# Causal masking by GpSimd instead of TensorE, and a reordered DMA queue, in a transformer layer kernel on one core

## The chip, the cores and the metric

The kernel runs on one core of one Trainium2 chip. The metric is device time in microseconds of the whole program, the median of several runs. The engines of a core are TensorE (PE in the profile, with PEld for its weight loads), VectorE (DVE), ScalarE (ACT), GpSimd (POOL) and SyncE (SP), which here only issues DMAs.

## The reference

One layer with modulated norms: attention with 16 heads of 32 over 4 batches of 1024 tokens and 512 features, then a gated feed-forward block of 2048 hidden features, all in float32. What matters here is the attention:

```python
scores = einsum('bhqd,bhkd->bhqk', qn, kn) / sqrt(hd)      # qn, kn: rotated, normalised heads
scores = where(causal, scores, finfo.min)
w = softmax(scores, axis=-1)
a = einsum('bhqk,bhkd->bhqd', w, v)
```

## The kernel before

The program is four stages one after the other: `qkv_stage`, `attention_stage`, `project_stage`, `ffn_stage`. Only `attention_stage` is touched.

It works on 16 groups (`NG`), each one batch and four heads. For a group, q and k are transposed on TensorE (`prepare`), widened by ScalarE (`widen`, into `whole`), split in a high and a low float32r part by GpSimd (`high`) and VectorE (`low`), and copied by 12 DMAs of 256 KB (`lay_stacks`, L705) into a stack whose rows let one matmul multiply both parts. A first pass of matmuls (`score`, L803) gives scores of which VectorE takes the maximum of each query (`peak`, L888 and L891); the maxima are transposed and laid as two more rows of the stack (`lay_peaks`). A second pass (`shift`, L821) gives scores less their maximum, keys on partitions and queries along the free axis, in PSUM tile `psB` with two buffers; ScalarE takes the exponential into `probT` (`exponent`, L961, three buffers of four heads); and TensorE multiplies it by v and by ones (`weigh`, L839), into `psO` and `psL`. Keys come in 8 blocks of 128 and queries in 2 halves of 512: 12 pairs (`BLOCKS`), of which 8 contain the diagonal. On those, `shift` adds a matmul of the mask with the identity (L824) to the 128 columns on the diagonal, in the same PSUM tile.

All engines walk the same list of steps k. `unit(k)` gives the round n and the step w from 0 to 11 in it. In round n, step w, the scores of group n are taken, two items a step. The shifts run 14 steps (`SHIFT_LAG`) behind, so block 0 of a group is shifted in step 2 of the round after; steps 2 to 5 and 10, 11, 0, 1 shift blocks on the diagonal, steps 6 to 9 blocks without it. A step on TensorE is: two shifts, four score matmuls, two shifts, then `prepare` (steps 1 and 3, for the group after), the transposition of maxima (step 0), then `weigh` of the block that was shifted one step earlier. The third shift waits for the first exponential of its step, the fourth for the second, since `psB` has two buffers. Score tiles and `prepare` share two slots of `psA`; a slot is free when VectorE (or ScalarE) has read what was in it.

SyncE's order in a round: `lay_peaks` in step 0, in step 4 `load` (q and k of the group two further) and all 12 transfers of `lay_stacks`, in step 5 `load_v`, in step 10 `store`. SyncE isn't held to the steps; only its waits hold it. On GpSimd `normalise` does, for each group but the last, in step 3 of the round two after the group's scores: one DMA of the four rows of sums to DRAM (L759), one back as a 128x32 tile (L761), a wait for VectorE's reciprocal (L937, step 8), one DMA of the inverses to DRAM (L763), four that broadcast them to 128 partitions (L766), and the product with the attention output (L769). GpSimd stands in `normalise` until all is done.

Of the kernel before, what the change touches and what calls it, by code (L numbers as in the profile page):

```python
# [20 lines left out]
F32 = mybir.dt.float32  # L21
# [556 lines left out]
def attention_stage(nc, args, scratch):  # L578
# [12 lines left out]
    BUFS = 3  # L591

# [19 lines left out]
    def weigh_at(k):  # L612
        return shift_at(k - 1)

# [16 lines left out]
    with ExitStack() as ctx:  # L631
# [3 lines left out]
        def sem(name):  # L635
# [20 lines left out]
        probT = sb("b_probT", [P, 3, 4, W])  # L656
# [9 lines left out]
                 "peaks_turned peaks_copied peaks_in shifted expd weighed summed taken_o taken_l sums_out few_in inverted few_out "  # L666
# [17 lines left out]
        def _(sp):  # L684
# [15 lines left out]
            def lay_stacks(n):  # L700
                at_least(sp, s["shifted"], 4 * NW * (n - BUFS + 1))
                sp.wait_ge(s["lo_done"], 2 * n + 2)
                for j in range(4):
                    for r, pair in enumerate((slice(0, 4, 3), slice(2, 4), slice(0, 2))):
                        sp.dma_start(stack[r * HD:(r + 1) * HD, n % BUFS, :, j].bitcast(F32),  # L705
                                     halves[j * HD:(j + 1) * HD, pair].bitcast(F32)).then_inc(stack_in[j], 16)
# [14 lines left out]

            load(0)
# [4 lines left out]
            for k in STEPS:  # L727
                n, w = unit(k)
                if peaks_at(k) is not None:
                    lay_peaks(peaks_at(k))  # L730
                if w == 4 and n + 2 < NG:
                    load(n + 2)
                if w == 4 and n + 1 < NG:
                    lay_stacks(n + 1)
                if w == 5 and 0 <= n < NG:
                    load_v(n)
                if w == 10 and 0 <= n - 2 < NG:
                    store(n - 2)
            sp.wait_ge(stored, 16 * NG)

        @block.gpsimd
        def _(pool):
            make_identity(nc, pool, ident, s["ident_ready"])
            pool.memset(ones[:], 1.0).then_inc(s["k_ones"], 1)
            for n in range(BUFS):
                pool.wait_ge(s["k_ones"], 1 + n)
                pool.memset(stack[ROWS:NR, n, 0].bitcast(F32), 1.0).then_inc(s["k_ones"], 1)
            pool.wait_ge(s["k_ones"], 1 + BUFS)

            def high(n, m):  # L750
                pool.wait_ge(s["whole"], 2 * n + m + 1)
                if m == 0:
                    for j in range(4):
                        at_least(pool, stack_in[j], 48 * n)
                pool.tensor_scalar(halves[:, 3 if m else 0], whole[:], 1.0, 1.0, ALU.mult, ALU.mult).then_inc(s["hi_done"], 1)

            def normalise(n):
                pool.wait_ge(s["taken_l"], 2 * n + 2)
                pool.dma_start(scratch["sums"][0], sums[0:P:HD, n % 2]).then_inc(s["sums_out"], 16)  # L759
                pool.wait_ge(s["sums_out"], 16 * n + 16)  # L760
                pool.dma_start(few[:, 0], scratch["sums"][0].rearrange("j (a c) -> (j a) c", c=C // HD)).then_inc(s["few_in"], 16)  # L761
                pool.wait_ge(s["inverted"], n + 1)
                pool.dma_start(scratch["sums"][1].rearrange("j (a c) -> (j a) c", c=C // HD), few[:, 1]).then_inc(s["few_out"], 16)  # L763
                pool.wait_ge(s["few_out"], 16 * n + 16)
                for j in range(4):
                    pool.dma_start(sums[j * HD:(j + 1) * HD, n % 2], scratch["sums"][1, j:j + 1].broadcast_to([HD, C])).then_inc(s["wide_in"], 16)  # L766
# [12 lines left out]
        def _(pe):  # L779
# [32 lines left out]
            def shift(n, w, j):  # L812
# [10 lines left out]
                if first == kb:  # L823
                    mm = pe.matmul(psB[:, i % 2, 0:P], mask_r[:], ident_r[:], start=False, stop=True, skip_group_check=True)  # L824
                mm.then_inc(s["shifted"], 1)

            def weigh(n, w, summing):
                half, kb = BLOCKS[w]
                if not summing:
                    pe.wait_ge(s["expd"], 4 * (NW * n + w) + 4)  # L830
                    if w == 0:
                        pe.wait_ge(s["v_in"], 16 * n + 16)
# [4 lines left out]
                for j in range(4):  # L837
                    rows = slice(j * HD, (j + 1) * HD)
                    mm = pe.matmul(out[rows, (first - half * HALF) * P:W], ones[:] if summing else v[:, n % 2, kb, rows],  # L839
                                   probT[:, (NW * n + w) % 3, j, 0:(half + 1) * W - first * P],  # L840
# [21 lines left out]
        def _(dve):  # L862
# [60 lines left out]
            for k in STEPS:  # L923
# [19 lines left out]
        def _(act):  # L943
# [9 lines left out]
            def exponent(n, w, j):  # L953
# [7 lines left out]
                act.activation(probT[:, (NW * n + w) % 3, j, 0:width], psB[:, i % 2, 0:width], ACT.Exp).then_inc(s["expd"], 1)  # L961
# [498 lines left out]
```

## Time and profile before

| | us |
|---|---|
| median of 3 runs | 2434.78 (2433.34 to 2436.04) |
| the profiled execution | 2436.47 |
| its span | 2434.3 |
| attention stage, within the span | about 400 to 1208 |
| TensorE busy | 2242.7 (92%) |
| VectorE, ScalarE, GpSimd busy | 1200.8, 792.2, 728.7 |

The span is from the first to the last instruction. Busy times of TensorE count a matmul from issue to the modelled end of its pipeline, so that neighbours overlap.

### The profile page before, as it was taken

Reading aid. Unit: us, or ns where it says so; the run is one execution under the profiler, and the core shown is the slowest. Engines: PE = TensorE matmul, PEld = TensorE weight load, DVE = VectorE, ACT = ScalarE, POOL = GpSimd, SP = SyncE. Lnnn points to the kernel's source line nnn. Section 1 sums busy time; section 2 is a strip of 40 time slices with the busy share of each in tenths; the row PEclk is TensorE's granted clock in tenths of the full one; section 3 lists DMA queues with packets and bytes.
Section 4 is the critical chain, followed back from the end, with each engine's and each line's share of the span. In section 5 each row is a group of like instructions: output and inputs, shape, how many; then the busy total and the mean of one; then the engine's idle time right before and its main releaser. Section 6 shows DMA issues by size and latency. Waiting matters only on the chain. (4 is left out here: it accounts for less than half of the span.)

```text
span 2434.3 us, 32672 instructions
## 1 busy us (share of the span) xinstructions
PE 2242.7 (92%) x12008; PEld 1649.6 (68%) x12008; DVE 1200.8 (49%) x2775; ACT 792.2 (33%) x1671; POOL 728.7 (30%) x694
## 2 busy tenths in 40 slices
PE   6999993799999999999678799999999999999998
PEld 3777771455555555555356588888888888888887
DVE  5999995566665665665279512222222222221212
ACT  3333331155555555555445411111111111111111
POOL 2677775002112112111277122222222222222221
PEclk8999996599999999999899899999999999999999
DMA  6222223555465465452288411212121211111111
GB/s 225 70 96 94 103 87 120 118 134 132 102 152 126 107 151 130 107 128 76 68 256 303 161 52 52 70 48 69 52 69 49 66 56 65 52 64 37 52 53 52
DMA packets 161834, 243.71 MB, mean 100 GB/s; under 512 B 17124, under 2 KB 84292, under 8 KB 161184
## 3 DMA queue, kind: packets, MB, share of 16 engines
q1 hardware_dynamic: 153184, 220.66, 31.0%
q0 software_dynamic: 7456, 18.07, 2.6%
q10 hardware_dynamic: 1056, 3.15, 0.3%
q8 instruction: 87, 1.43, 0.2%
q14 instruction: 51, 0.42, 0.1%
HBM read 131.69 MB, written 59.26 MB: 78 GB/s over the span
## 5 line engine op out<-in xcount | busy, mean ns | idle before, releaser
L1324 DVE TENSOR_TENSOR f_gu<-f_psU,f_silu 128x512 f32<-128x512 f32 x128 | 88.6, 692 | 712.3 <-PE f_psU L1391 712.3
L961 ACT ACTIVATE b_probT<-b_psB 128x512 f32<-128x512 f32 (+3 forms) x768 | 339.4, 490 | 300.0 <-PE b_psB L824 220.9
L891 DVE TENSOR_REDUCE b_top<-b_psA 128x2 f32<-128x1024 f32 (+2 forms) x320 | 288.6, 902 | 134.0 <-PE b_psA L803 133.8
L1280 POOL TENSOR_SCALAR f_wd_hi<-f_wd 128x512 fp32r<-128x512 f32 x128 | 83.4, 652 | 819.7 <-PE f_psD L1376 775.9
L821 PE MATMUL b_psB<-b_stack 98*128 98x512 f32 (+3 forms) x768 | 273.6, 401 | 5.1 <-ACT b_probT L961 4.6
L821 PEld LDWEIGHTS b_psB<-b_stack 98*128 98x128 f32 x768 | 141.4, 189 | 156.0 <-issue 103.2
L1300 ACT ACTIVATE f_silu<-f_psG 128x512 f32<-128x512 f32 x128 | 76.5, 598 | 504.2 <-PE f_psG L1391 504.2
L803 PE MATMUL b_psA<-b_stack 96*128 96x512 f32 (+3 forms) x768 | 193.5, 373 | 35.8 <-DMA b_stack<-b_halves 20.1
L1389 PE MATMUL f_psG<-f_hT_hi,w_hi 128*128 128x512 f32 x512 | 200.4, 391 | 11.0 <-DVE f_hT_lo L1318 11.0
L1391 PE MATMUL f_psG<-f_hT_lo,w_hi 128*128 128x512 f32 x512 | 199.9, 390 | 0.0
L1390 PE MATMUL f_psG<-f_hT_hi,w_lo 128*128 128x512 f32 x512 | 199.9, 390 | 0.0
L1295 ACT ACTIVATE f_gu_hi<-f_gu 128x512 fp32r<-128x512 f32 x128 | 80.9, 632 | 364.5 <-DVE f_gu L1324 364.5
L1390 PE MATMUL f_psU<-f_hT_hi,w_lo 128*128 128x512 f32 x512 | 199.2, 389 | 0.0
L1391 PE MATMUL f_psU<-f_hT_lo,w_hi 128*128 128x512 f32 x512 | 199.2, 389 | 0.0
L1389 PE MATMUL f_psU<-f_hT_hi,w_hi 128*128 128x512 f32 x512 | 199.2, 389 | 0.0
L1374 PE MATMUL f_psD<-f_wd_hi,f_gu_hi 128*128 128x512 f32 x512 | 199.2, 389 | 0.0
L1375 PE MATMUL f_psD<-f_wd_lo,f_gu_hi 128*128 128x512 f32 x512 | 199.2, 389 | 0.0
L1376 PE MATMUL f_psD<-f_wd_hi,f_gu_lo 128*128 128x512 f32 x512 | 199.2, 389 | 0.0
L803 PEld LDWEIGHTS b_psA<-b_stack 96*128 96x128 f32 x768 | 136.2, 200 | 65.9 <-issue 22.6
L1282 POOL TENSOR_TENSOR f_wd_lo<-f_wd,f_wd_hi 128x512 fp32r<-128x512 f32 x128 | 168.8, 1319 | 10.7
L839 PE MATMUL b_psO<-b_probT,b_v 128*32 128x512 f32 (+3 forms) x1536 | 165.4, 503 | 0.0
L839 PE MATMUL b_psL<-b_probT,b_ones 128*32 128x512 f32 (+3 forms) x1536 | 159.0, 486 | 0.0
(178 smaller groups left out, 4084.4 us busy)
## 6 DMA issues: line engine op xcount, KB each, us to landing
b_stack<-b_halves SPq DMA_DIRECT2D x192, 256.0 KB, 5.1
f_wd<-in_wd_t SPq DMA_DIRECT2D x128, 256.0 KB, 2.6
qkv_d<-a_t SPq DMA_DIRECT2D x32, 512.0 KB, 2.7
b_land<-qkv_d SPq DMA_DIRECT2D x32, 512.0 KB, 4.7
a_x<-in_x SPq DMA_DIRECT2D x32, 256.0 KB, 3.3
qkv_d<-a_v SPq DMA_DIRECT2D x32, 256.0 KB, 3.1
b_v<-qkv_d SPq DMA_DIRECT2D x16, 512.0 KB, 5.8
att_d<-b_att SPq DMA_DIRECT2D x16, 512.0 KB, 3.2
```

The costliest lines, as they stand in the source:

```text
L803: mm = pe.matmul(out[:, h, 0:hi - lo], stack[0:ROWS, n % BUFS, 1, j, t * P:(t + 1) * P], stack[0:ROWS, n % BUFS, 0, j, lo:hi], start=True, ...
L821: mm = pe.matmul(psB[:, i % 2, cols], stack[0:NR, n % BUFS, 0, j, kb * P:(kb + 1) * P], stack[0:NR, n % BUFS, 1, j, first * P:(half + 1) * ...
L839: mm = pe.matmul(out[rows, (first - half * HALF) * P:W], ones[:] if summing else v[:, n % 2, kb, rows], probT[:, (NW * n + w) % 3, j, 0:(h ...
L891: last = dve.tensor_reduce(into, tile[:, :, 0:width], AX.X, ALU.max, negate=True)
L961: act.activation(probT[:, (NW * n + w) % 3, j, 0:width], psB[:, i % 2, 0:width], ACT.Exp).then_inc(s["expd"], 1)
L1282: pool.tensor_tensor(wd_lo[:, u % 2], wd[:, u % 2], wd_hi[:, u % 2].bitcast(F32), ALU.subtract).then_inc(s["wd_lo"], 1)
L1374: pe.matmul(out_t, gu_hi[:, u % 2, cols], wd_hi[:, u % 2], start=first, stop=False)
L1375: pe.matmul(out_t, gu_hi[:, u % 2, cols], wd_lo[:, u % 2], start=False, stop=False)
L1376: mm = pe.matmul(out_t, gu_lo[:, u % 2, cols], wd_hi[:, u % 2], start=False, stop=end)
L1389: pe.matmul(out_c, w_hi[:, m, k, cols], hi, start=(k == 0), stop=False)
L1390: pe.matmul(out_c, w_lo[:, m, k, cols], hi, start=False, stop=False)
L1391: mm = pe.matmul(out_c, w_hi[:, m, k, cols], lo, start=False, stop=(k == KC - 1))
```

## The change

In the diagonal blocks the mask matmul is gone. ScalarE takes the exponential of the unmasked values, and GpSimd clears those above the diagonal in `probT` with one `affine_select` over the four heads' 128x128 squares (`cut`); `weigh` waits for the cut in diagonal blocks, and for the exponential in the others. The DMAs of `normalise` move from GpSimd's queue to SyncE's, with their waits; what is left on GpSimd is the wait for the broadcast and the product, now in two halves, in step 10. VectorE's reciprocal moves from step 8 to 7. `lay_stacks` is called once a head from steps 4 to 7, `load_v` goes from step 5 to 7, `store` from step 10 to step 1 of the round after. `PROBS = 3` names the number of `probT` buffers, which stays.

```diff
+    DIAGONAL = [w for w, (half, kb) in enumerate(BLOCKS) if kb >= half * HALF]
+    def cut_at(k):
+        at = shift_at(k)
+        return at if at and at[1] in DIAGONAL else None
...
-            def lay_stacks(n):
-                at_least(sp, s["shifted"], 4 * NW * (n - BUFS + 1))
-                sp.wait_ge(s["lo_done"], 2 * n + 2)
-                for j in range(4):
-                    for r, pair in enumerate((slice(0, 4, 3), slice(2, 4), slice(0, 2))):
-                        sp.dma_start(stack[r * HD:(r + 1) * HD, n % BUFS, :, j].bitcast(F32),
-                                     halves[j * HD:(j + 1) * HD, pair].bitcast(F32)).then_inc(stack_in[j], 16)
+            def lay_stacks(n, j):
+                if j == 0:
+                    at_least(sp, s["shifted"], 4 * NW * (n - BUFS + 1))
+                    sp.wait_ge(s["lo_done"], 2 * n + 2)
+                for r, pair in enumerate((slice(0, 4, 3), slice(2, 4), slice(0, 2))):
+                    sp.dma_start(stack[r * HD:(r + 1) * HD, n % BUFS, :, j].bitcast(F32),
+                                 halves[j * HD:(j + 1) * HD, pair].bitcast(F32)).then_inc(stack_in[j], 16)
...
+            def sums_out(n):
+                sp.wait_ge(s["taken_l"], 2 * n + 2)
+                sp.dma_start(scratch["sums"][0], sums[0:P:HD, n % 2]).then_inc(s["sums_out"], 16)
+            def few_in(n):
+                sp.wait_ge(s["sums_out"], 16 * n + 16)
+                sp.dma_start(few[:, 0], scratch["sums"][0].rearrange("j (a c) -> (j a) c", c=C // HD)).then_inc(s["few_in"], 16)
+            def few_out(n):
+                sp.wait_ge(s["inverted"], n + 1)
+                sp.dma_start(scratch["sums"][1].rearrange("j (a c) -> (j a) c", c=C // HD), few[:, 1]).then_inc(s["few_out"], 16)
+            def wide_in(n):
+                sp.wait_ge(s["few_out"], 16 * n + 16)
+                for j in range(4):
+                    sp.dma_start(sums[j * HD:(j + 1) * HD, n % 2], scratch["sums"][1, j:j + 1].broadcast_to([HD, C])).then_inc(s["wide_in"], 16)
...
-                if w == 4 and n + 1 < NG:
-                    lay_stacks(n + 1)
-                if w == 5 and 0 <= n < NG:
+                if 0 <= n - 2 < NG - 1 and w in (4, 5, 8, 9):
+                    {4: sums_out, 5: few_in, 8: few_out, 9: wide_in}[w](n - 2)
+                if 4 <= w < 8 and n + 1 < NG:
+                    lay_stacks(n + 1, w - 4)
+                if w == 7 and 0 <= n < NG:
                     load_v(n)
-                if w == 10 and 0 <= n - 2 < NG:
-                    store(n - 2)
+                if w == 1 and 0 <= n - 3 < NG:
+                    store(n - 3)
...
+            def cut(n, w):
+                pool.wait_ge(s["expd"], 4 * (NW * n + w) + 4)
+                square = probT[:, (NW * n + w) % PROBS, :, 0:P]
+                pool.affine_select(out=square, in_=square, compare_op=ALU.is_ge, fill=0.0, base=0,
+                                   pattern=[[0, 4], [1, P]], channel_multiplier=-1).then_inc(s["cut"], 1)
             def normalise(n):
-                (the seven DMAs with their waits)
                 pool.wait_ge(s["wide_in"], 64 * n + 64)
                 pool.wait_ge(s["taken_o"], 2 * n + 2)
-                pool.tensor_tensor(att[:, n % 2], att[:, n % 2], sums[:, n % 2], ALU.mult).then_inc(s["scaled"], 1)
+                for half in range(2):
+                    cols = slice(half * W, (half + 1) * W)
+                    mul = pool.tensor_tensor(att[:, n % 2, cols], att[:, n % 2, cols], sums[:, n % 2, cols], ALU.mult)
+                mul.then_inc(s["scaled"], 1)
             for k in STEPS:
+                if cut_at(k):
+                    cut(*cut_at(k))
                 if prep_at(k):
                     high(*prep_at(k))
-                at = take_at(k)
-                if at and at[1] == 1 and at[0] < NG - 1:
-                    normalise(at[0])
+                n, w = unit(k)
+                if w == 10 and 0 <= n - 2 < NG - 1:
+                    normalise(n - 2)
...
-                if first == kb:
-                    mm = pe.matmul(psB[:, i % 2, 0:P], mask_r[:], ident_r[:], start=False, stop=True, skip_group_check=True)
...
-                    pe.wait_ge(s["expd"], 4 * (NW * n + w) + 4)
+                    if w in DIAGONAL:
+                        pe.wait_ge(s["cut"], len(DIAGONAL) * n + DIAGONAL.index(w) + 1)
+                    else:
+                        pe.wait_ge(s["expd"], 4 * (NW * n + w) + 4)
...
-                at = take_at(k - 5)
-                if at and at[1] == 1 and at[0] < NG - 1:
-                    dve.wait_ge(s["few_in"], 16 * at[0] + 16)
+                n, w = unit(k)
+                if w == 7 and 0 <= n - 2 < NG - 1:
+                    dve.wait_ge(s["few_in"], 16 * (n - 2) + 16)
                     dve.reciprocal(few[:, 1], few[:, 0]).then_inc(s["inverted"], 1)
```

## Rows read from the trace of the kernel before

**Rows 1.** Window of 50 us; busy PE, PEld, DVE, ACT, POOL, PEclk, DMA share, GB/s.

```profile
630.00:680.00 50.00, 48.57 (x369) 29.11 (x367) 31.83 (x109) 28.32 (x61) 8.12 (x10) 1.00 0.57 136
```

**Rows 2.** Timeline of SyncE's DMA issues: loads, stacks and v, and the next loads.

```profile
621.48 1.00 SPq L693 DMA_DIRECT2D b_land<-qkv_d  x2
625.22 13.72 SPq L705 DMA_DIRECT2D b_stack<-b_halves  x12
638.99 1.23 SPq L698 DMA_DIRECT2D b_v<-qkv_d  x1
...
667.20 1.00 SPq L693 DMA_DIRECT2D b_land<-qkv_d  x2
```

**Rows 3.** Timeline of TensorE: start us, us, instruction, [idle before <- releaser]; transposes.

```profile
612.26 1.06 PE L788 MATMUL b_psA<-b_ident,b_land 128*128 128x128 f32 x8 [0.44 <-DVE b_top L891]
...
620.36 1.09 PE L788 MATMUL b_psA<-b_ident,b_land 128*128 128x128 f32 x8 [0.66 <-DVE b_top L891]
```

**Rows 4.** Timeline of TensorE: starts of steps 1, 9, 10, 11, and weighings.

```profile
609.90 0.33 PE L821 MATMUL b_psB<-b_stack 98*128 98x128 f32 x1
...
610.40 1.02 PE L803 MATMUL b_psA<-b_stack 96*128 96x384 f32 x4
...
640.12 0.73 PE L821 MATMUL b_psB<-b_stack 98*128 98x512 f32 x2
640.70 0.87 PE L803 MATMUL b_psA<-b_stack 96*128 96x512 f32 x4
...
642.23 1.07 PE L839 MATMUL b_psO<-b_probT,b_v 128*32 128x512 f32 x8
...
644.08 0.50 PE L821 MATMUL b_psB<-b_stack 98*128 98x512 f32 x1
644.42 0.23 PE L824 MATMUL b_psB<-b_ident_r,b_mask_r 128*128 128x128 f32 x1
644.48 0.45 PE L821 MATMUL b_psB<-b_stack 98*128 98x512 f32 x1
...
644.83 1.03 PE L803 MATMUL b_psA<-b_stack 96*128 96x512 f32 x4
...
646.43 1.06 PE L839 MATMUL b_psO<-b_probT,b_v 128*32 128x512 f32 x8
...
648.28 0.44 PE L821 MATMUL b_psB<-b_stack 98*128 98x384 f32 x1
...
650.51 1.06 PE L839 MATMUL b_psO<-b_probT,b_v 128*32 128x512 f32 x8
...
654.19 0.85 PE L839 MATMUL b_psO<-b_probT,b_v 128*32 128x384 f32 x8
```

**Rows 5.** Timelines of VectorE and TensorE around the scores of step 5.

```profile
626.61 0.69 DVE L891 TENSOR_REDUCE b_top<-b_psA 128x2 f32<-128x512 f32 x1
...
627.07 1.14 PE L803 MATMUL b_psA<-b_stack 96*128 96x512 f32 x4
```

**Rows 6.** Timeline of the weight loads: the fourth shift of step 9.

```profile
641.79 0.19 PEld L821 LDWEIGHTS b_psB<-b_stack 98*128 98x128 f32 x1 [0.30 <-ACT b_probT L961]
```

**Rows 7.** Groups of GpSimd: busy us, mean ns | idle before: the select of 128x128.

```profile
L108 POOL TENSOR_SCALAR_AFFINE_SELECT b_ident<-b_ident 128x128 f32<-128x128 f32 x1 | 0.3, 294 | 0.1
```

**Rows 8.** Timeline of ScalarE: the last two exponentials of step 10.

```profile
646.19 1.09 ACT L961 ACTIVATE b_probT<-b_psB 128x512 f32<-128x512 f32 x2 [0.43 <-PE b_psB L824]
```

**Rows 9.** Window of 2 us, columns as in rows 1, while the stacks are transferred.

```profile
630.00:632.00 2.00, 2.00 (x23) 1.29 (x22) 1.58 (x10) 1.83 (x4) 0.00 (x0) 1.00 0.99 211
```

**Rows 10.** The instructions of L705, the stack transfers: from issue to landing.

```profile
DMA to landing us min/median/max: 3.2/5.1/7.1
```

**Rows 11.** Timeline of GpSimd: inverses out, broadcast in, product.

```profile
639.60 0.55 POOL L763 DMA_DIRECT2D sums_d<-b_few  x1 [11.85 <-DVE b_few L937]
643.12 1.98 POOL L766 DMA_DIRECT2D b_sums<-sums_d  x4 [2.97 <-DMA sums_d<-b_few]
647.62 2.38 POOL L769 TENSOR_TENSOR b_att<-b_att,b_sums 128x1024 f32<-128x1024 f32 x1 [2.53 <-DMA b_sums<-sums_d]
```

More of the change, by code:

```diff
@@ L591, in attention_stage @@
     BUFS = 3
+    PROBS = 3
     def unit(k):
@@ L655, in attention_stage @@
         peak_rows = sb("b_peak_rows", [8 * TB, P])
-        probT = sb("b_probT", [P, 3, 4, W])
+        probT = sb("b_probT", [P, PROBS, 4, W])
         sums = sb("b_sums", [P, 2, C])
@@ L665, in attention_stage @@
         names = ("mask_in ln_ready whole ident_ready consts k_ones qk_in v_in turned hi_done lo_done scored maxed peaks_ready "
-                 "peaks_turned peaks_copied peaks_in shifted expd weighed summed taken_o taken_l sums_out few_in inverted few_out "
+                 "peaks_turned peaks_copied peaks_in shifted expd cut weighed summed taken_o taken_l sums_out few_in inverted few_out "
                  "wide_in scaled end_inverted end_scaled").split()
@@ L755, in high @@
                 pool.tensor_scalar(halves[:, 3 if m else 0], whole[:], 1.0, 1.0, ALU.mult, ALU.mult).then_inc(s["hi_done"], 1)
-            def normalise(n):
[L758 to L766, printed above, removed]
+            def cut(n, w):
[3 more added lines that the diff above has]
+                                   pattern=[[0, 4], [1, P]], channel_multiplier=-1).then_inc(s["cut"], 1)
+            def normalise(n):
                 pool.wait_ge(s["wide_in"], 64 * n + 64)
                 pool.wait_ge(s["taken_o"], 2 * n + 2)
-                pool.tensor_tensor(att[:, n % 2], att[:, n % 2], sums[:, n % 2], ALU.mult).then_inc(s["scaled"], 1)
+                for half in range(2):
+                    cols = slice(half * W, (half + 1) * W)
+                    mul = pool.tensor_tensor(att[:, n % 2, cols], att[:, n % 2, cols], sums[:, n % 2, cols], ALU.mult)
+                mul.then_inc(s["scaled"], 1)
             for k in STEPS:
+                if cut_at(k):
+                    cut(*cut_at(k))
                 if prep_at(k):
                     high(*prep_at(k))
-                at = take_at(k)
-                if at and at[1] == 1 and at[0] < NG - 1:
-                    normalise(at[0])
+                n, w = unit(k)
+                if w == 10 and 0 <= n - 2 < NG - 1:
+                    normalise(n - 2)
         @block.tensor
@@ L839, in weigh @@
                     mm = pe.matmul(out[rows, (first - half * HALF) * P:W], ones[:] if summing else v[:, n % 2, kb, rows],
-                                   probT[:, (NW * n + w) % 3, j, 0:(half + 1) * W - first * P],
+                                   probT[:, (NW * n + w) % PROBS, j, 0:(half + 1) * W - first * P],
                                    start=(kb == 0), stop=(kb == (half + 1) * HALF - 1), skip_group_check=True)
@@ L960, in exponent @@
                 width = (half + 1) * W - max(kb, half * HALF) * P
-                act.activation(probT[:, (NW * n + w) % 3, j, 0:width], psB[:, i % 2, 0:width], ACT.Exp).then_inc(s["expd"], 1)
+                act.activation(probT[:, (NW * n + w) % PROBS, j, 0:width], psB[:, i % 2, 0:width], ACT.Exp).then_inc(s["expd"], 1)
             def copy_peaks(n):
```

## The prediction, made before the changed kernel ran

> **What bounds the kernel now.** I read the windows of the attention stage first, since every edit lies there (400 to 1205 us of the span). TensorE is busy 97% of a 50 us window, VectorE, ScalarE and GpSimd 64, 57 and 16%, at a granted clock of 1.00, the 2.4 GHz level [rows 1]. So TensorE's order of work sets the pace, but a busy TensorE row includes pipelining; what counts is where it waits, which the timeline tells. One round of twelve steps takes 45.7 us: SyncE's loads of step 4 are issued at 621.48 and at 667.20 [rows 2]. All times below are of the round from 609.90 to 655.6. TensorE waits for VectorE in it, 0.44 us before the transposes of step 1 and 0.66 us before those of step 3 [rows 3]. These two transpose blocks are 8.10 us apart (612.26 to 620.36), and between them lies a chain with no mask matmul in it: transposes, ScalarE widen, GpSimd high, VectorE low, VectorE maxima.
>
> **Mask matmuls removed.** 8 of 12 blocks are diagonal, 4 heads each, 16 groups: 512 matmuls with their weight loads. Price of one: in step 10 the two first shifts take 644.08 to 644.83, 0.75 us with two masks; the same pair without, in step 9, 640.12 to 640.70, 0.58 us [rows 4]. The stream itself is 0.06 us (644.42 to 644.48), the rest is its weight load. That is 0.09 us; narrower blocks, where the load weighs more, I put at 0.09 to 0.115 (the pair of 128 columns in step 1 takes 0.50 us, 609.90 to 610.40, and I put it at 0.27 without). Were TensorE alone the bound: 512 x 0.095 = 48.6 us. That is the upper end. The Trainium skill (TensorE: Matmul & The Clock Gate, Back-to-back issue gap) gives some 81 ns as the sustained spacing of a 128-column load-and-matmul pair, so 41.5 us by the page; the trace's 0.09 is near it; neither says how much is kept.
>
> How much is kept, step by step. Steps 2 and 3 and the second pair of step 1 (10 masks): nothing, they lie inside waits or inside the 8.10 us chain that VectorE ends. Step 1, first pair: 0.50 becomes 0.27, the scores, the maxima and the transposes move up by 0.23. Step 4: 0.38. Step 5: its first pair gains 0.19 more, but its second score, at 627.50 before (0.43 into the scores of 627.07), would be issued 0.61 earlier, and its PSUM slot is free only when the VectorE reduce of 626.61 ends (0.69 us, 627.30) [rows 5]. That chain starts at the transposes of step 3, so 0.14 is left at that point and the second pair adds 0.20: steps 4 and 5 keep 0.34. Steps 6 to 9 have no mask. Step 10: without masks the fourth shift waits for ScalarE as in step 9 (the weight load idles 0.30 us) [rows 6], and weighing starts 2.11 us after the step in place of 2.35: 0.24. Step 11: 384 columns, exponentials shorter, so ScalarE holds nothing; weighing 2.23 us after 648.28; I keep 0.36. Step 0: 0.30 of 0.38, the rest to the exponentials. Sum 0.34 + 0.24 + 0.36 + 0.30 + 0.23 = 1.47 us a round, 15 rounds: **22 us gained**. Beyond the last scores ScalarE sets the pace; I take 0 there.
>
> **GpSimd cuts added.** 128 of them, 4x128 elements a partition. A select of 128x128 took 0.294 us [rows 7]. Lower bound that row itself, upper four times it, 1.18; the element work grows by four and only the start is paid once, so I take 0.9, nearer to the upper end. TensorE now waits for the cut where it waited for the fourth exponential. What is queued behind that wait is all of TensorE's stream, and ScalarE and VectorE wait for that. But the weighing of a block comes a whole step later: the exponentials of step 10 end at 647.28 (646.19 + 1.09) and its weighing is at 650.51 [rows 4, 8], 3.2 us later, 2.6 without the masks between; step 0's end about as long before the weighing in step 1. So a cut of 0.9, even of 1.2, is hidden, if GpSimd is free. The cut goes ahead of `high`, but `high` waits for ScalarE's widen, 1.2 us long and behind the same exponentials: hidden too. The last block has no step behind it: 0.9 us once, I put the tail at +1.
>
> **Transfers moved to SyncE.** The DMA engines are full from 624 to 642 us (0.99 of their time and 211 GB/s at 630 to 632) [rows 9]. SyncE issues 2 loads at 621.48, 12 stack transfers at 625.22 taking 13.72 us together, v at 638.99 for 1.23 [rows 2]. SyncE is not paced by steps, only by its waits, so "four steps" is only an order: new is loads, `sums_out` (behind the loads), three stacks, `few_in` (wait passed), nine stacks, v, `few_out`, wait, four `wide_in`. `few_in` is issued near 627.6 and lands some 5.1 us later, the stacks' median [rows 10], near 633; the reciprocal, now in step 7, is reached near 635 (the inverses of step 8 left at 639.60, a step is 3.96): no wait. `few_out` in the kernel before was issued at 639.60 from GpSimd's own queue, as soon as VectorE's reciprocal was there, and the four `wide_in` followed at 643.12 [rows 11]. Now it waits for SyncE: 625.22 + 13.72 + 0.6 (`few_in`) + 1.23 = 640.8. It stands behind v in the same queue; the stack transfers there take 3.2 / 5.1 / 7.1 us from issue to landing, so 644.0 to 647.9, I take 645.9. From the first `wide_in` to the product it was 4.5 us (643.12 to 647.62), so the product starts near 650.4 in place of 647.62. It lasts 2.4 us (in two halves). **The new wait:** on GpSimd the product of step 10 stands ahead of the cut of step 11, and it waits for `wide_in`. So that cut runs 652.8 to 653.7. TensorE wants it in step 0: 654.19 before, less 0.34 + 0.24 + 0.36 + 0.30 = 652.95. It waits about 0.7 us a round, in the 13 rounds that have both a product and stack transfers: **9 us given back**. The other queue effects are covered: the stacks are needed a half round later, `lay_peaks` at 654.62 stands behind `wide_in` issued by 648, v is needed a round on, the store moved to step 1 has until step 7.
>
> The Trainium skill (DMA: Bandwidth & Descriptors, Queues, rings and completion order) says that an engine consumes one ring in order and takes turns between rings. By that rule small transfers behind megabytes on SyncE's queue wait for them, and on GpSimd's own queue they did not: 3.5 us for `few_out` (639.60 to 643.12) against 5.1 for a stack on the full queue agrees. It speaks against this part of the change.
>
> **Sum.** 2436.47 (profiled execution: span 2434.3 and 2.2 around it) - 22 + 9 + 1 = 2424.5. The median shown is 1.7 lower, so 2422.8; I say 2423.
>
> **Rivals.** (a) The landing is earlier, or the cut shorter by 0.3, and the wait at step 0 vanishes: 0.7 us is little against DMA spreads of 4 us. Then 2434.8 - 21 = 2414, and if step 5 and ScalarE hold back less than I say, 2404. For it: SyncE's four issues may be quicker than GpSimd's. Against: full DMA engines. (b) GpSimd, stuck at the product, becomes the bound. One wait, `wide_in` at step 10 ahead of the next cut: it decides from a product start of 651.2, where the stall eats the 1.47. If `few_out` takes the 7.1 us of the longest stack transfer, the product starts at 652.4: 2.7 us of wait a round, 13 x 2.7 = 35 against 21, 2449 us; with 6.2 us, 2438. For it: the ring order above. Against: the queue drains behind v. (c) The masks were wholly covered (VectorE and ScalarE chains already set each step) and the wait as well: 2433 to 2436, no change. Against: steps 4, 11 and 0 have no idle entry before their shifts or scores.
>
> **How the numbers follow.** A median of this kernel can be told apart from no change at about 0.2%, 5 us: faster is below 2429.9. Forecast (2416 to 2430, a wait of 0.2 to 1.3 us): 0.48. (a) 0.22. (c) 0.12. (b) 0.18. Range 2404 to 2442 takes in (a) whole and (b) up to a landing of 6.6 us, leaving out about 2 in 10. Faster 0.47 + 0.22 = 0.69, same 0.14, slower 0.17.
>
> **What would show it.** No row of a mask matmul; a pair of 512-column shifts at 0.56 to 0.60 us in step 10. The two transpose blocks of a round still 8.1 us apart. Cuts at 0.5 to 1.2 us. `few_out` issued after v, 15 to 16 us after the first stack, the product 25 us after the first stack. A wait of TensorE for the GpSimd cut once a round, at the weighing of step 0, near 0.7 us; if it is 0, (a), if above 1.5, (b). A round of 45.7 - 1.47 + 0.7 = 44.9 us. Wrong altogether: cuts over 2 us, a VectorE wait for `few_in`, or a TensorE wait at another cut.

## The result, and the profile after

The changed kernel took 2422.94 us (median of 6 runs, 2422.32 to 2426.79) against 2434.94 (6 runs, 2433.34 to 2436.04): a ratio of 0.9953, interval 0.9942 to 0.9964. The forecast was 2423. The size is right, and so is the 22 us gained; the reason given for the 9 us given back is not.

The profiled span is 2423.7 us. The first view is the page's table of busy times: TensorE is down from 2242.7 us (512 instructions fewer). GpSimd is up by 27: 81.1 us of cuts came, and 55.7 us of issuing the DMAs of `normalise` went. The second is the grouped view of two GpSimd lines, the cut and the product: how many, ns of one as least/median/most, and the first and last start.

```profile
PE 2211.0 (91%) x11496; PEld 1588.9 (66%) x11496; DVE 1207.5 (50%) x2775; ACT 790.4 (33%) x1671; POOL 755.8 (31%) x732
```

```profile
L786 POOL TENSOR_SCALAR_AFFINE_SELECT b_probT<-b_probT x128: 625/634/642, 479.6 to 1189.1; 128x512 f32<-128x512 f32 x128
...
L794 POOL TENSOR_TENSOR b_att<-b_att,b_sums x30: 1268/1280/1294, 558.7 to 1181.8; 128x512 f32<-128x512 f32 x30
```

TensorE's timeline after, answering to [rows 3, 4]: the two transposition blocks, and the two first shifts of step 10.

```profile
611.56 1.06 PE L816 MATMUL b_psA<-b_ident,b_land 128*128 128x128 f32 x8 [0.66 <-DVE b_top L920]
...
619.65 1.09 PE L816 MATMUL b_psA<-b_ident,b_land 128*128 128x128 f32 x8 [0.83 <-DVE b_top L920]
...
643.05 0.73 PE L849 MATMUL b_psB<-b_stack 98*128 98x512 f32 x2
643.62 0.98 PE L831 MATMUL b_psA<-b_stack 96*128 96x512 f32 x4
```

The blocks are still 8.09 us apart, with longer waits before them (0.66 and 0.83 for 0.44 and 0.66): what the masks of steps 1 to 3 cost inside that chain became waiting. The pair of step 10 takes 0.57 us, not 0.75.

SyncE's timeline after, answering to [rows 2, 11].

```profile
624.51 2.35 SPq L712 DMA_DIRECT2D b_stack<-b_halves  x3
626.91 1.17 SPq L735 DMA_DIRECT2D b_few<-sums_d  x1
628.13 10.04 SPq L712 DMA_DIRECT2D b_stack<-b_halves  x9
638.22 1.24 SPq L705 DMA_DIRECT2D b_v<-qkv_d  x1
639.50 1.47 SPq L739 DMA_DIRECT2D sums_d<-b_few  x1
644.88 1.72 SPq L744 DMA_DIRECT2D b_sums<-sums_d  x4
```

`few_out` went 15.0 us after the first stack transfer and the broadcast 5.4 us after it. Now the three engines at that place: GpSimd, then VectorE's gathering of the maxima (L926 to L933), then TensorE.

```profile
646.02 0.63 POOL L786 TENSOR_SCALAR_AFFINE_SELECT b_probT<-b_probT 128x512 f32<-128x512 f32 x1 [17.41 <-ACT b_probT L990]
649.14 2.52 POOL L794 TENSOR_TENSOR b_att<-b_att,b_sums 128x512 f32<-128x512 f32 x2 [2.48 <-DMA b_sums<-sums_d]
651.61 0.64 POOL L786 TENSOR_SCALAR_AFFINE_SELECT b_probT<-b_probT 128x512 f32<-128x512 f32 x1
```

```profile
649.69 0.96 DVE L920 TENSOR_REDUCE b_top<-b_psA 128x2 f32<-128x768 f32 x1
650.68 1.02 DVE L926 TENSOR_TENSOR b_least<-b_top 128x32 f32<-128x32 f32 x1
651.74 0.55 DVE L928 SCALAR_TENSOR_TENSOR b_least<-b_corner,b_least 128x32 f32<-128x32 f32 x1
652.32 0.18 DVE L931 CAST b_peaks<-b_least 128x32 fp32r<-128x32 f32 x1
652.54 0.19 DVE L933 TENSOR_TENSOR b_peaks<-b_least,b_peaks 128x32 fp32r<-128x32 f32 x1
652.66 0.29 DVE L917 CUSTOM_DVE_ANT_0 b_masked<-b_psA,b_mask 128x128 f32<-128x128 f32 x1
```

```profile
651.56 0.66 PE L849 MATMUL b_psB<-b_stack 98*128 98x256 f32 x2
653.32 0.30 PE L838 MATMUL b_psA<-b_ident,b_peaks 128*128 128x128 f32 x1 [1.10 <-DVE b_corner L917]
653.55 0.85 PE L868 MATMUL b_psO<-b_probT,b_v 128*32 128x384 f32 x8
```

The product starts 24.6 us after the first stack transfer, as forecast (25.2), and the cut behind it ends at 652.25. But TensorE stands somewhere else, one instruction earlier: at the transposition of the maxima (L838), for 1.10 us. Its weights are what L933 writes, and its PSUM slot comes free by maxima that VectorE takes behind L933. The four small operations of the gathering are late, and two of them are long: L926 took 1.02 us, and it ended when the second half of the product ended (651.7); L928 took 0.55 and ended with the cut. The grouped view of the same two lines shows what they took before (they are L897 and L899 there) and after, ns as least/median/most:

```profile
L897 DVE TENSOR_TENSOR b_least<-b_top x16: 191/191/216, 467.2 to 1154.4; 128x32 f32<-128x32 f32 x16
...
L899 DVE SCALAR_TENSOR_TENSOR b_least<-b_corner,b_least x16: 191/191/193, 467.5 to 1154.6; 128x32 f32<-128x32 f32 x16
```

```profile
L926 DVE TENSOR_TENSOR b_least<-b_top x16: 191/399/1024, 468.0 to 1144.6; 128x32 f32<-128x32 f32 x16
...
L928 DVE SCALAR_TENSOR_TENSOR b_least<-b_corner,b_least x16: 191/370/1205, 468.2 to 1144.8; 128x32 f32<-128x32 f32 x16
```

In the view of waits of the kernel after (total us, times, longest), this wait and the one that I had forecast:

```profile
PE b_psA L838 <- DVE b_corner L917: 7.7, 12, 1.8
...
PEld b_psO L868 <- POOL b_probT L786: 0.6, 1, 0.6
```

One of the twelve (0.6 us, in the first round) is there before too, so 7.1 us in 11 rounds are new; the wait for the cut came once. There is a second loss, seen in windows of 4 us (columns as in [rows 1]): in some rounds TensorE's granted clock falls.

```profile
528.00:532.00 4.00, 3.17 (x17) 1.96 (x20) 1.59 (x6) 1.84 (x3) 0.64 (x1) 0.61 0.02 7
532.00:536.00 4.00, 4.00 (x36) 1.81 (x28) 2.68 (x5) 1.48 (x5) 1.45 (x2) 0.96 0.92 270
```

The same engine, with the same work, stands near its lower level of 1.2 GHz (a granted clock of 0.5) for most of a window, after the waits around the transposition block of step 3. It isn't the new wait that comes before this fall: the transposition of the maxima at 517.00 waited for nothing. Such a round is 1.1 us longer here: 45.83 us from 517.00 to 562.83 with a wait of 0.27, against 44.93 from there to 607.76 with one of 0.47. The kernel before had two such falls (at 756 and 940 us, about 1.6 us each), this one has four (528, 664, 888, 980). All six come about 12 us behind the transposition of the maxima. Falls behind the last scores, where these kernels have one or none, are left out of all counts here.

### The profile page after: what moved, and what is told of

Read it like the earlier page. It is cut to its first block and busy times, and to the rows that moved or that the text cites. A ratio compares the mean times of both kernels' runs of the same rounds, so it can differ in the third digit from the quotient of the medians.

```text
span 2423.7 us, 31792 instructions
## 1 busy us (share of the span) xinstructions
PE 2211.0 (91%) x11496; PEld 1588.9 (66%) x11496; DVE 1207.5 (50%) x2775; ACT 790.4 (33%) x1671; POOL 755.8 (31%) x732
## 5 line engine op out<-in xcount | busy, mean ns | idle before, releaser
L849 PE MATMUL b_psB<-b_stack 98*128 98x512 f32 (+3 forms) x768 | 253.8, 397 | 6.8 <-ACT b_probT L990 6.8
L849 PEld LDWEIGHTS b_psB<-b_stack 98*128 98x128 f32 x768 | 131.1, 189 | 171.1 <-issue 106.5
L786 POOL TENSOR_SCALAR_AFFINE_SELECT b_probT<-b_probT 128x512 f32<-128x512 f32 x128 | 81.1, 634 | 486.6 <-ACT b_probT L990 486.6
```

The lines of the kernel that those rows point to most:

```text
L849: mm = pe.matmul(psB[:, i % 2, cols], stack[0:NR, n % BUFS, 0, j, kb * P:(kb + 1) * P], stack[0:NR, n % BUFS, 1, j, first * P:(half + 1) * ...
```

## The experiments

The ratios below are against the kernel before, run on the same chip. Theory P is that VectorE's gathering is held by GpSimd's instructions; Q is the prediction's own, queueing on GpSimd or a full DMA ring.

**Masks left out, nothing cleared.** The kernel before without its mask matmuls, to see what their removal alone is worth.

```diff
-                if first == kb:
-                    mm = pe.matmul(psB[:, i % 2, 0:P], mask_r[:], ident_r[:], start=False, stop=True, skip_group_check=True)
```

> The kernel before with the 512 mask matmuls left out and nothing in their place (values above the diagonal are not cleared); transfers and product stay where they were. It prices the mask matmuls alone. Prediction on record: 1.47 us kept in each of 15 rounds, 22 us, so 2413. Reading of the changed kernel's trace: 37.6 us from the transposes of step 3 to those of the next step 1 became 36.4 where nothing waited, 1.25 us a round, 19 us, so 2416; the 8.10 us from the transposes of step 1 to those of step 3 stay. If VectorE and ScalarE covered the masks wholly: 2433 to 2436. If TensorE alone set the pace: 2386.

2410.7 us (2409.63 to 2415.68), ratio 0.9907 (0.9891 to 0.9922). It is 24.3 us under before. A round takes 44.35 us in place of 45.70: 1.35 kept, where I summed 1.47. Over the 13 full rounds that is 17.6; the last, from the 15th transposition of maxima to the 16th, which has no chain with transposes, gives 2.4 (41.81 to 39.37), the first 1.8 (48.15 to 46.33; a part of this may be the clock, which comes back to its upper level in this round, at 483.5 us and not at 484.6), and the two falls of the clock are gone, 3.2. That is 25.0 of the 25.7 us between the two spans. The median lies under both forecasts above (2413 and 2416), since neither had the falls. So the changed kernel gives back 12 us of what removing masks is worth.

**Transfers alone.** The change, with the masks back and the cuts gone.

```diff
+                if first == kb:
+                    mm = pe.matmul(psB[:, i % 2, 0:P], mask_r[:], ident_r[:], start=False, stop=True, skip_group_check=True)
...
-                if cut_at(k):
-                    cut(*cut_at(k))
...
-                    if w in DIAGONAL:
-                        pe.wait_ge(s["cut"], len(DIAGONAL) * n + DIAGONAL.index(w) + 1)
-                    else:
-                        pe.wait_ge(s["expd"], 4 * (NW * n + w) + 4)
+                    pe.wait_ge(s["expd"], 4 * (NW * n + w) + 4)
```

> The changed kernel with the mask matmuls back and no cuts: only the transfers on SyncE, the reciprocal in step 7, the halved product in step 10 and the later store. Theory Q (what I forecast: the product, waiting for the broadcast, holds the next cut and TensorE waits for that cut): without cuts nothing waits, no change against before, within 2 us. Theory P (VectorE's two-input operations of the gather in step 0 are held while a GpSimd operation on SBUF runs): the product ends 27 us after the first stack transfer, the gather of a round with masks comes at about the same time (652.2 against 651.6 in the round I use), so a few rounds are hit by a part of an operation: 0 to 3 us slower. Q and P hardly differ here; the run tells whether the transfers cost anything without the cuts.

2434.54 us (2432.51 to 2436.65), ratio 0.9997 (0.9988 to 1.0006): the reordered queue alone neither gives nor takes. The product starts where it does in the change (649.53 us in this round, for 2.52), but with rounds of 45.7 us the gathering comes only at 652.25, 0.2 us behind its end; in 13 of 16 rounds its first operation takes 0.19 us. In two rounds TensorE waits for it, 0.18 and 0.11 us. So the late product does harm that counts only together with the shorter round.

**The product in step 2.** All of the change, but the product goes a third of a round later, to step 2, behind that step's cut, and the store with it to step 3. From the second round on, the last cut before the gathering then ends 0.3 us before it (in one round 602.86 and 603.18).

```diff
-                if w == 10 and 0 <= n - 2 < NG - 1:
-                    normalise(n - 2)
+                if w == 2 and 0 <= n - 3 < NG - 1:
+                    normalise(n - 3)
...
-                if w == 1 and 0 <= n - 3 < NG:
+                if w == 3 and 0 <= n - 3 < NG:
                     store(n - 3)
```

> The changed kernel, with the product of a group in step 2 of the round after, behind that step's cut, and its store in step 3. No cut stands behind a wait for the broadcast, and the product runs 34 us away from the gather. Theory Q: the wait of TensorE at the weighing of step 0 goes; as its trace shows only 0.6 us of that wait in all, 0 to 1 us faster than the changed kernel, 2422. Theory P: gather operations back at 0.19 us each, the waits of TensorE before the transposition of the maxima (7.1 us in all) go, 6 to 8 us faster than the changed kernel: 2415 to 2417. Against both: if the product delays the cut of step 3, a wait appears there.

2411.95 us (2410.63 to 2413.36), ratio 0.9905 (0.9889 to 0.992): 11 us under the changed kernel, more than P asked for. In the grouped view the gathering is back at 191 ns in all 16 rounds, and in the view of waits only the first round's entry is left:

```profile
L926 DVE TENSOR_TENSOR b_least<-b_top x16: 191/192/193, 466.2 to 1130.5; 128x32 f32<-128x32 f32 x16
...
L928 DVE SCALAR_TENSOR_TENSOR b_least<-b_corner,b_least x16: 191/191/193, 466.4 to 1130.7; 128x32 f32<-128x32 f32 x16
```

```profile
PE b_psA L838 <- DVE b_corner L917: 0.6, 1, 0.6
```

Rounds take 44.35 us again. It is within 1.3 us of the kernel that clears nothing, so the 128 cuts (81 us of GpSimd) cost nearly nothing by themselves (the profiled spans are 3.0 us apart, with one fall of the clock here in the full rounds and none there). Of the 12.1 us between this span (2411.6) and the changed kernel's, 7.1 are the waits, 1.2 some 0.11 us more in each of those 11 rounds, and 3.3 three falls of the clock more at 1.1 (this kernel has one).

**The cut first.** The product moved from step 10 to step 11, behind that step's cut. By the prediction's mechanism this is the cure: the cut waits for no transfer any more. By P it is the worst place, with both halves right beside the gathering.

```diff
-                if w == 10 and 0 <= n - 2 < NG - 1:
+                if w == 11 and 0 <= n - 2 < NG - 1:
                     normalise(n - 2)
```

> The changed kernel, with the product in step 11, behind the cut of that step in place of ahead of it. The one wait that theory Q is about is taken away: by Q 2422 or faster, down to 2414 if the forecast 0.7 us a round had been right. By theory P the product now begins after that cut, just when VectorE gathers the maxima, in every round: the gather's first operation is held 0.9 to 1.2 us and the second 1.0 to 1.3 us, TensorE waits 1.5 to 2.2 us a round before the transposition, where it waited 0.5 on average: 1.0 to 1.7 us x 13 rounds, 13 to 22 us slower than the changed kernel, 2436 to 2445.

2458.09 us (2456.84 to 2459.38), ratio 1.0098 (1.0082 to 1.0113): slower than before, and 35 us slower than the change. The cure makes it worse. GpSimd's, VectorE's and TensorE's timelines of one round:

```profile
651.90 0.64 POOL L786 TENSOR_SCALAR_AFFINE_SELECT b_probT<-b_probT 128x512 f32<-128x512 f32 x1 [3.06 <-ACT b_probT L990]
652.50 2.50 POOL L794 TENSOR_TENSOR b_att<-b_att,b_sums 128x512 f32<-128x512 f32 x2
654.96 0.63 POOL L786 TENSOR_SCALAR_AFFINE_SELECT b_probT<-b_probT 128x512 f32<-128x512 f32 x1
```

```profile
652.87 0.96 DVE L926 TENSOR_TENSOR b_least<-b_top 128x32 f32<-128x32 f32 x1
653.86 1.19 DVE L928 SCALAR_TENSOR_TENSOR b_least<-b_corner,b_least 128x32 f32<-128x32 f32 x1
655.08 0.54 DVE L931 CAST b_peaks<-b_least 128x32 fp32r<-128x32 f32 x1
655.66 0.19 DVE L933 TENSOR_TENSOR b_peaks<-b_least,b_peaks 128x32 fp32r<-128x32 f32 x1
```

```profile
656.44 0.30 PE L838 MATMUL b_psA<-b_ident,b_peaks 128*128 128x128 f32 x1 [2.03 <-DVE b_corner L917]
```

Read the ends: the halves of the product end near 653.8 and 655.0 and the cut at 655.6, and L926, L928 and L931 end at 653.83, 655.05 and 655.62. Each operation of VectorE gets through when one of GpSimd ends, and is then held by the next. The wait is 2.03 us in each of 13 rounds, 26.4 us. P's 2436 to 2445 was too low since it had no price for the clock, which now falls 12 times, in nine of the 13 rounds (in three of them twice): 47.60 us for the round that ends at 656.44, but 46.48 for the one that ends at 798.14 with the same wait and no fall, so 1.12 us each.

**The product in eighths.** Step 10 as in the change, with eight instructions of 128 columns in place of two of 512. If the two engines share bandwidth, the size of the pieces doesn't matter; if they take turns by whole instructions, the longest hold gets shorter.

```diff
-                for half in range(2):
-                    cols = slice(half * W, (half + 1) * W)
+                for half in range(8):
+                    cols = slice(half * P, (half + 1) * P)
```

> The changed kernel, product in its place (step 10), but in eight instructions of 128 columns in place of two of 512. If a GpSimd instruction holds VectorE's two-input operations until it ends (theory P as the run with the product in step 11 showed it, 0.96 and 1.19 us beside instructions of 1.25), a gather operation now waits for at most one piece, 0.35 to 0.45 us: none of them over 0.65 us, waits of TensorE before the transposition of the maxima down from 7.1 to 3 to 5 us in all, although the product is longer (8 pieces of some 0.4, 3.2 us in place of 2.5): 0 to 4 us faster than the changed kernel, 2419 to 2423. If the two engines share bandwidth in place of taking turns, the piece size doesn't matter, and the longer product makes it slower: the waits 8 to 10 us, 2424 to 2427.

2427.69 us (2423.67 to 2428.01), ratio 0.9961 (0.9948 to 0.9975); span 2423.3, as the change. The grouped view and the waits:

```profile
L926 DVE TENSOR_TENSOR b_least<-b_top x16: 191/266/459, 467.2 to 1144.2; 128x32 f32<-128x32 f32 x16
...
L928 DVE SCALAR_TENSOR_TENSOR b_least<-b_corner,b_least x16: 191/378/551, 467.4 to 1144.5; 128x32 f32<-128x32 f32 x16
...
L794 POOL TENSOR_TENSOR b_att<-b_att,b_sums x120: 449/459/494, 555.9 to 1181.6; 128x128 f32<-128x128 f32 x120
```

```profile
PE b_psA L838 <- DVE b_corner L917: 8.5, 14, 0.8
```

An operation of the gathering took at most 0.46 us beside pieces of the product and 0.56 beside a cut, where it had been 1.20, and the longest wait fell from 1.8 us to 0.8. Each held operation again ends within 0.06 us of the end of a GpSimd instruction (649.40 and 649.35, 649.82 and 649.77 in one round): turns by whole instructions. The total did not fall, though, from 7.1 to 7.9 us, against 3 to 5 expected: the product now takes 3.38 us in all, so it meets the gathering in more rounds and holds more of its four operations (median of L933 0.39 us, 0.19 in the change). It also ends later, and the wait that the prediction spoke of shows at last: TensorE waits for the cut before a weighing in three places more than in the change, 0.3 to 0.8 us each. By sum and time the forecast for shared bandwidth (8 to 10 us of waits, 2424 to 2427) came nearer than that of P; it is the lengths and ends of the held operations that speak for turns. The mechanism was read rightly, the size missed.

**A shorter chain.** The product in step 2 leaves the 8.10 us chain as the largest wait. Three things of VectorE's lie in it: `low`, the copy of the attention output (`take`), and the maxima. First the copy goes behind the first maxima of its step, in steps 3 and 7.

```diff
-                if take_at(k):
-                    take(*take_at(k))
                 for i in range(2):
                     if score_at(k):
                         n, w = score_at(k)
                         peak(n, 2 * w + i)
+                    if i == 0 and take_at(k):
+                        take(*take_at(k))
```

> The run with the product in step 2 (2411.95), with VectorE's copy of the attention output (0.61 to 0.69 us) behind the first maxima of its step in place of ahead of them. It tests the part of the forecast that nothing of the masks is kept in steps 1 to 3 because VectorE ends the chain between the transposes. If VectorE's order does set these 8.10 us, the transposes of step 3 come 0.6 us sooner (distance 7.5, TensorE's wait before them 0.83 down to 0.23), a round is 43.75 us in place of 44.35: 14 rounds, 8 us faster, 2404. If TensorE would be late by itself just behind (its scores, or ScalarE's exponentials), 0 to 3 us: 2409 to 2412.

2431.87 us (2426.97 to 2434.92), ratio 0.9979 (0.997 to 0.9988): 20 us above the higher of the two forecasts. The chain is 8.00 us, and a new wait appears in step 7, where the next half's weighing needs `psO` as soon as the shifts are out (TensorE's timeline):

```profile
633.41 1.06 PE L868 MATMUL b_psO<-b_probT,b_v 128*32 128x512 f32 x8 [0.79 <-DVE b_att L939]
```

It comes in every round, 13.4 us in sum. There are five falls of the clock now, and the last part, with one of them in it, is 3.9 us longer.

**And `low` later.** As the last, and `low` goes behind the first maxima of the step after.

```diff
+                    if i == 0 and prep_at(k - 1):
+                        low(*prep_at(k - 1))
                     if i == 0 and take_at(k):
                         take(*take_at(k))
...
-                if prep_at(k):
-                    low(*prep_at(k))
```

> The run before it, and VectorE's low parts behind the first maxima of the step after the transposes, where VectorE idled 2.4 and 2.9 us a round for GpSimd's high parts. If the idle time is what the chain consists of, the maxima of step 2 are done 0.4 us sooner and the chain is another 0.4 us shorter: 14 x 0.4, 5 to 6 us faster than the run before, 2398. The scores of that step are written only 0.4 us before the high part is ready, so not more. If the low part, now later by 0.8 us, is late for ScalarE's next widen or for the stacks, no gain or a loss: 2404 to 2410.

2416.54 us (2415.68 to 2417.99), ratio 0.992 (0.9906 to 0.9933). It is above both forecasts (2398, or 2404 to 2410). The chain is 7.20 us now and the clock holds, but the 13.4 us of the copy are still there. So the copies gave the loss, and `low` may be worth moving. Two runs take the edits apart.

**`low` alone.** The copy is back ahead of the maxima.

```diff
+                    if i == 0 and prep_at(k - 1):
+                        low(*prep_at(k - 1))
...
-                if prep_at(k):
-                    low(*prep_at(k))
```

> Product in step 2 behind the cut, as in the experiment that ran at 2411.95 us, and of the two VectorE moves tried since only one: the low parts of the prepared tiles go behind the first maxima of the next step, while the copy of the attention output stays ahead of the maxima. Theory P (the stretch from the transposes of step 1 to those of step 3 is a chain that VectorE ends, so work taken out of it comes back as time, and what spoiled the two later versions is only TensorE's wait for the copy of psO, 13.4 us): the transposes are 7.3 to 7.6 us apart in place of 8.10, no wait for the copy, about 0.6 us a round over 14 rounds less: 2401 to 2405. Theory Q (with the copy ahead of the maxima the chain is as long as it was, only its last member has changed): transposes 8.0 to 8.1 apart, 2410 to 2413.

2408.77 us (2408.13 to 2410.36), ratio 0.9891 (0.9875 to 0.9906). Between P and Q: the transposes are 7.80 us apart in every round, 0.30 less, and the waits for the copy are gone. But a round is no shorter, 44.40 us for 44.35. `low` is moved twice in a round, and behind the block of step 3 it now stands ahead of maxima that TensorE's next scores need. TensorE's timelines with the product in step 2, and with `low` later:

```profile
623.52 0.73 PE L831 MATMUL b_psA<-b_stack 96*128 96x512 f32 x2 [0.25 <-DVE b_top L920]
```

```profile
620.14 0.73 PE L831 MATMUL b_psA<-b_stack 96*128 96x512 f32 x2 [0.58 <-DVE b_top L920]
```

The 0.30 us come back as 0.33 of waiting. The 3 us by which the run is faster lie elsewhere: the first transposition of maxima is 2.2 us earlier (465.40 and 467.61), a fall of the clock is gone (1.0), and the part behind the last transposition is 2.0 us shorter.

**The copy of step 7 alone.** This kernel was meant to move the copy of step 3; it moves that of step 7, so its expectation answers another question.

```diff
-                if take_at(k):
+                if take_at(k) and take_at(k)[1] == 1:
                     take(*take_at(k))
...
+                    if i == 0 and take_at(k) and take_at(k)[1] == 0:
+                        take(*take_at(k))
```

> As the run with the low parts behind the first maxima, but the copy of the attention output is put behind the first maxima in step 3, where it lies inside the chain, and stays ahead of them in step 7, where TensorE waited 0.79 us for it. Theory P (the wait of the weighing for the copy arises in step 7 alone, and the copy in step 3 costs the chain its 0.61 us): transposes 7.0 to 7.2 apart, wait for the copy under 2 us in all, 2396 to 2402 and 3 to 6 us under its sister. Theory Q (the copy is late in step 3 too, or the chain is then set by ScalarE and GpSimd): no more than 2 us away from its sister, or behind it.

2430.08 us (2426.4 to 2436.3), ratio 0.9976 (0.9966 to 0.9986). It prices the wait of step 7 by itself: 12.1 us of waiting for the copy, but 21 us of time against the run before, of which five falls of the clock, at 1.6 us, are 8. A round without a fall of the clock is 45.27 us against 44.40, and every other one from 700 us on is 46.9.

**The copy of step 3 alone.** The two conditions of the last diff exchanged.

```diff
-                if take_at(k):
+                if take_at(k) and take_at(k)[1] == 0:
                     take(*take_at(k))
...
+                    if i == 0 and take_at(k) and take_at(k)[1] == 1:
+                        take(*take_at(k))
```

> The run before this one put the copy of step 7 behind the maxima, not that of step 3 as its expectation said: half 1 ends in step 3, half 0 in step 7. Here it is the copy of step 3, and the one of step 7 stays ahead. Theory P (the wait of the weighing for the copy arises in step 7 alone, and the copy in step 3 costs the chain its 0.61 us): transposes 7.1 to 7.3 apart in place of 7.80, no wait for the copy, 44.40 less 0.6 in 14 rounds: 2399 to 2403 with the masks cleared. Theory Q (the chain is then set by another member, or the time gained before step 3 is lost behind it, where VectorE is late with the scores of step 3): within 3 us of 2408.77.

2404.53 us (2401.1 to 2405.27), ratio 0.9874 (0.9857 to 0.989), the fastest of all, 30 us under before and 18 under the change. P is borne out for the round, 0.6 us shorter than with `low` alone. The median is 1.5 us above its range, and only 4.2 us of the 7.8 that 13 such rounds give are there: by the two profiles the first round and the last are longer by 1.4 us each (48.39 for 47.01, 40.74 for 39.40), and what follows them by 2.0. Why isn't known. TensorE's timeline of the two blocks:

```profile
605.00 1.06 PE L816 MATMUL b_psA<-b_ident,b_land 128*128 128x128 f32 x8 [0.66 <-DVE b_top L920]
...
612.21 1.09 PE L816 MATMUL b_psA<-b_ident,b_land 128*128 128x128 f32 x8 [0.28 <-DVE b_top L920]
```

7.21 us apart in place of 8.10, and a round of 43.80 us in place of 45.70. The moves add up in an odd way: both copies alone took 0.10 us off the chain, `low` alone 0.30, and `low` with the copy of step 3 0.89.

## Why the prediction was right, and where it was wrong

**The masks: right, a little large.** 1.35 us a round and not 1.47, for 13 full rounds and not 15; with the first and the last round, 1.8 and 2.4, the stage gives 21.8 us, and 22 were forecast. That the two errors nearly cancel is luck. That the masks of steps 2 and 3 would bring nothing held to the hundredth, as the unchanged 8.10 us show. What I didn't count is the two falls of the clock in the kernel before, 3.2 us, which are gone in the first experiment. One reading of the sum I can't find again: no row has 627.50 for the second score of step 5. Its first matmul, the third of the four from 627.07, starts at 627.59, 0.29 us after its slot is free at 627.30, where I took 0.14 us of room. With 0.29 the sum would have been larger, and further from 1.35.

**The cuts: right.** 0.634 us against 0.9, and hidden. By itself the product's new place costs nothing either (the transfers alone, ratio 0.9997).

**The queue: right, with one wrong consequence.** `few_out` landed in 4.8 us (median; 5.1 taken), the product came 24.6 us after the first stack (25.2). From these I had the cut of step 11 end 28.5 us after the first stack transfer, and TensorE want it at 27.7. It ended at 27.7 (652.25 less 624.51: product 0.6 earlier, cut 0.26 shorter) and TensorE wanted it at 27.9 (653.55 less 1.10). The 0.7 us never came; on this wait rival (a) was right, which would have given 2414 us.

**The 9 us given back: the failed step.** The step was the sentence "It waits about 0.7 us a round", at the weighing of step 0, for the cut. What was really given back is 11 to 12 us, by another route: the same product, moved beside VectorE's gathering, and the cut right behind it hold up to four operations of 0.19 us of which nothing in the forecast speaks, and TensorE waits for those: 7.1 us in 11 rounds, 0.65 a round where it occurs. Three more falls of the clock took 3.3 us besides. Both routes begin with a late product in step 10, cost near 0.7 us a round where they occur and fall in step 0; so the forecast came out within 0.1 us of the median by luck. The run that cures my mechanism (the cut first) is 35 us slower, and the one that cures the other is 11 us faster.

What in the profile of before could have told, VectorE's timeline, a row that I hadn't read for the forecast:

```profile
652.18 0.19 DVE L897 TENSOR_TENSOR b_least<-b_top 128x32 f32<-128x32 f32 x1
```

The product ended at 650.00 [rows 11], 2.2 us before it. By my own figures it would now run from 650.4 to 652.8, and the gathering would come at 652.18 less the 1.2 us that steps 4 to 0 had gained: one across the other. The sum priced GpSimd's new work by who waits for its results. It didn't ask who else is slowed while it runs. The Trainium skill (SBUF — State Buffer, "Who interferes with whom") has the rule: the ports of GpSimd to SBUF are VectorE's second pair, and whoever has the pair keeps it for a whole instruction while the other stands. VectorE wants it for two inputs in SBUF, beside a GpSimd instruction that reads SBUF, and in its two-port modes, which a cast can enter. The traces show who is held and until when, not the ports, and in this they agree: L926 and L928 have two inputs in SBUF and were held, up to 1.20 us beside a product half of 1.28; the cast L931 went from 0.18 to 0.54 beside a cut; L917 and the reduces, which read their data from PSUM, kept their 0.28 and 0.96 us in the same microseconds. The reverse, GpSimd held by VectorE, isn't seen in the changed kernel: its 128 cuts took 0.625 to 0.642 us, and its 30 product halves 1.268 to 1.294.

**The rivals.** (b) needs a product start of 651.2 or later and didn't come about by itself; its size did, a wait above 1.5 us a round, by the other mechanism and at another place, in the run with the cut first. (c) is refuted by the first experiment.

**Still open.** Why the clock falls in one round and not in another with the same waits. More waiting goes with more falls in part of the runs (none in the full rounds of the first experiment, four in the change, 12 with 2.03 us of wait each round). But the kernel before has two without the new wait, and of two runs with the same 13.4 us of waits for the copy one has five and the other, with `low` later too, has none. The runs only show what one costs.

## What to carry to other kernels

When work moves to GpSimd, or in time on GpSimd, list what VectorE does in those microseconds, not only who waits for the result: a chain of tiny VectorE operations with both inputs in SBUF is held by each GpSimd instruction in turn, and if TensorE's next instruction hangs on it, every such hold is the kernel's time. Here, moving the long GpSimd instruction to where VectorE mostly reads PSUM gave 11 us, and cutting it in pieces gave none. And when a chain bounds a stretch, move its members one at a time, and read the length of the round and not only that of the chain: of three moves that looked alike, one took 0.6 us off a round, one took 0.3 off the chain and nothing off the round, and one cost 21 us in all.

## What the hardware showed that I had not expected

- The hold is by whole instructions: operations of 0.19 us took up to 1.20 us beside instructions of 1.28, and at most 0.56 beside pieces of 0.46 and cuts of 0.63.
- TensorE's clock can fall for 3 to 4 us in a stage that otherwise runs at 1.00. One fall costs 1.1 to 1.6 us (1.0 in one run), and five of them are 8 of the 21 us that 12.1 us of waits for the copy cost.
- Clearing a 128x(4x128) tile by a select on GpSimd takes 0.634 us, about twice the 0.294 of one of 128x128 [rows 7], not four times.
